# Fused cross-attention and layer norm: five tiles score q as projected, q's copies are issued early and then in one row, buffers of loads and stores are re-cut

## The reference

```
q = x @ wq;  k = ctx @ wk;  v = ctx @ wv            (split into 16 heads of 32)
scores = q . k / sqrt(32), masked with -inf where the mask is set
attn = softmax(scores) @ v
out = attn @ wo + x
result = (out - mean) / sqrt(var + 1e-5) * gamma + beta      (over the 512 columns)
```

## Time and profile before

| | |
|---|---|
| median of 3 runs | 668.11 us (665.15 to 670.7) |
| profiled execution, its own time | 671.11 us |
| its span in the trace | 668.9 us |
| PE busy | 619.7 us (93%) |
| DVE, ACT, POOL busy | 529.3, 507.7, 495.9 us |
| mean granted clock of TensorE | 0.977 |

### The profile page before, as it was taken

One profiled execution on the slowest core, in us unless ns is written; L12 is line 12 of the kernel. 1 busy time (PEld: TensorE's weight loads), 2 busy tenths in 40 slices (PEclk: granted clock), 3 DMA queues, 4 the chain that ended last, 5 costly groups with the idle time before them and its releaser, 6 DMA issues.

```text
span 668.9 us, 12812 instructions
## 1 busy us (share of the span) xinstructions
PE 619.7 (93%) x3836; PEld 481.1 (72%) x3836; DVE 529.3 (79%) x1007; ACT 507.7 (76%) x1558; POOL 495.9 (74%) x640
## 2 busy tenths in 40 slices
PE   7899499898998999999999999999999999999995
PEld 5667268586786868878786868777777868777663
DVE  5657359687787888888887889888888888888887
ACT  4757368687787878888887879888887879787761
POOL 6456336677696887979797887979797898867785
PEclk9799699999999999999999999999999999999999
DMA  8831725436264453717264453727273553727112
GB/s 293 229 97 20 190 58 138 130 102 185 78 174 153 111 157 95 221 57 220 87 182 145 122 147 113 203 65 219 80 195 121 140 147 96 210 88 188 34 48 111
DMA packets 56531, 91.14 MB, mean 136 GB/s; under 512 B 10896, under 2 KB 13968, under 8 KB 56464
## 3 DMA queue, kind: packets, MB, share of 16 engines
q1 hardware_dynamic: 56464, 90.32, 46.7%
HBM read 39.53 MB, written 16.78 MB: 84 GB/s over the span
## 4 chain that ended last, share of the span: by engine, by line
PE 44%; SPq 14%; DVE 14%; POOL 12%; DMA 7%; issue 5%; ACT 3%; POOLq 0%; DVEq 0%; ACTq 0%
PE bank L374 14%; PE bank L469 12%; SPq L280 10%; DMA qd<-qn 5%; PE bank L441 4%; PE bank L410 3%; PE bank L420 3%; POOL pn L888 3%; POOL y L912 3%; POOL y L914 3%; PE bank L396 2%; PE bank L446 2%; DVE pr L721 2%; DVE sm L734 2%; SPq L258 2%
## 5 line engine op out<-in xcount | busy, mean ns | idle before, releaser
L582 ACT ACTIVATE pr<-pr,nm 128x77 f32<-128x77 f32 x1024 | 269.9, 348 | 71.4 <-DVE nm L727 68.6
L888 POOL TENSOR_TENSOR pn<-pr,rec 128x512 f32<-128x512 f32 x128 | 134.9, 1054 | 117.4 <-DVE rec L736 110.5
L721 DVE SCALAR_TENSOR_TENSOR pr<-msk,bank 128x308 f32<-128x308 uint8 x256 | 111.0, 469 | 64.4 <-PE bank L410 49.9
L410 PE MATMUL bank<-kd,qd 128*128 128x154 f32 x480 | 85.9, 261 | 25.3 <-DMA qd<-qn 25.3
L469 PE MATMUL bank<-woh,ah 128*128 128x512 f32 x256 | 104.2, 407 | 3.7 <-DVE ql L709 2.3
L374 PE MATMUL bank<-xh,wqh 128*128 128x512 f32 x256 | 107.3, 419 | 0.0
L734 DVE TENSOR_REDUCE sm<-pr 128x8 f32<-128x616 f32 x128 | 99.7, 779 | 7.6 <-ACT pr L582 6.5
L727 DVE TENSOR_REDUCE nm<-pr 128x8 f32<-128x616 f32 x128 | 101.8, 795 | 4.4
L549 ACT ACTIVATE ptr<-bank 128x512 f32<-128x512 f32 (+1 forms) x256 | 95.7, 427 | 10.1 <-PE bank L420 9.9
L374 PE MATMUL bank<-xh,wql 128*128 128x512 f32 x256 | 102.3, 400 | 0.0
L374 PE MATMUL bank<-xl,wqh 128*128 128x512 f32 x256 | 102.3, 399 | 0.0
(11 more groups left out here) (75 smaller groups left out, 991.6 us busy)
## 6 DMA issues: line engine op xcount, KB each, us to landing
qd<-qn SPq DMA_DIRECT2D x240, 128.0 KB, 2.4
xraw<-xT SPq DMA_DIRECT2D x59, 256.0 KB, 3.0
xres<-x SPq DMA_DIRECT2D x58, 256.0 KB, 2.8
out<-y SPq DMA_DIRECT2D x56, 256.0 KB, 2.0
zt<-x SPq DMA_DIRECT2D x6, 256.0 KB, 3.9
out<-zt SPq DMA_DIRECT2D x6, 256.0 KB, 2.0
ptr<-xT SPq DMA_DIRECT2D x5, 256.0 KB, 9.0
kd<-kh SPq DMA_DIRECT2D x8, 154.0 KB, 3.6
```

What stands on the lines that cost most here:

```text
L410: last = nc.tensor.matmul(o[:, u * PW:(u + 1) * PW], qd[:, g, u, r * P:(r + 1) * P], kd[:, g, u, t // TB, :], start=False, stop=(u == 1))
L582: last = nc.scalar.activation(s, s, ACT.Exp, bias=nm[:, t % 2, h:h + 1], scale=1.0)
L721: nc.vector.scalar_tensor_tensor(out=pr[:, 4 * g:4 * g + 4, :], in0=msk[:, b % 2, t % TB, :].unsqueeze(1).broadcast_to([P, 4, LK]), scalar ...
L888: nc.gpsimd.tensor_tensor(pn[:, half, 0:4, :].rearrange("p s (e k) -> p (s e) k", e=2), pr[:, hs, 0:KM], rec[:, t % 2, hs].unsqueeze(2).br ...
```

## The change

- `kt` gets its own tile (`kt_sb`), placed so that it shares memory with the fourth group of `qd` and with `qn`. Its batch-0 part alone is cleared, by VectorE and not by GpSimd, and `pair_k` copies just the two blocks of 32 rows that hold data, with two transfers in place of one.
- Tiles 0 to 4 (PLAIN = 4) score q as projected. The four groups of block 1 are doubled one by one in SP's iterations 1 to 4 (DOUBLES), the fourth after tile 4's scores; for block 2 `keep_q` waits for tile 4's scores.
- From block 2 on all sixteen transfers of a block are issued in one row, after the load of a slice and before the store.
- NX goes from 3 to 2 and YS from 2 to 3. Slice t + 9 is loaded in iteration t. Slices 2 and 3 at the start go to other places.
- `place_v` is spread over iterations 0, 2, 4 and 5, one batch each. gamma and beta are loaded in iteration 5. The loads for the residual go ahead of `place_v` in iteration 5 and wait for the projection of v (`p_v`).
- The wait for the last of `place_v` moves from `project_o(0)` on TensorE to `standardise(0)` on ScalarE. `keep_q(3)` goes ahead of a slice and the first exponentials. `mask_all` runs in tiles with t % 16 = 1, before 2.

```diff
-NX = 3
-YS = 2
+NX = 2
+YS = 3
+
+PLAIN = 4
...
+DOUBLES = {1: 4, 2: 5, 3: 6, 4: 7}
+
-PLACE = {0: 0, 2: 1, 5: 2}
+PLACE = {0: (0, 0), 2: (1, 1), 4: (2, 1), 5: (3, 2)}
...
+            early("place_xres", [P, 4 * D - KT * NB * LK])
             vs = early("vs", [P, 3, 4, 2, 2, HD])
+        with ExitStack() as second:
+            second.enter_context(nc.sbuf_tensor("below_kt", [P, 6 * D], f32))
+            kt_sb = second.enter_context(nc.sbuf_tensor("kt_sb", [P, NB, NG, PW], f32r))
...
+        xres = sb("xres", [P, XR, D])
         y = sb("y", [P, YS, D])
-        xres = sb("xres", [P, XR, D])
...
                 sp.wait_ge(v_k, 4 * g + 4)
-                sp.dma_start(kd[64:128, g, 0].bitcast(f32), kt[0:64, g].bitcast(f32)).then_inc(d_kd[g], 16)
+                for j in range(2):
+                    sp.dma_start(kd[64 + 32 * j:96 + 32 * j, g, 0, :, j * LK:(j + 1) * LK].bitcast(f32),
+                                 kt[32 * j:32 * j + 32, g, :, j * LK:(j + 1) * LK].bitcast(f32)).then_inc(d_kd[g], 16)
...
-                sp.wait_ge(p_s, NG * (4 * blk - 1) + m + 1)
-                if i == 4:
-                    for g in range(NG):
-                        sp.wait_ge(d_kd[g], 48)
+                if blk > 1:
+                    sp.wait_ge(p_s, NG * (4 * blk - 1) + m + 1)
+                elif m == NG - 1:
+                    sp.wait_ge(p_s, NG * (PLAIN + 1))
                 sp.wait_ge(a_qh, i + 1)
...
-            for n in range(8, 11):
+            for n in range(8, 10):
                 load_slice(n)
...
             for t in range(T + LAG):
-                if t % 4 == 3 and t < T - 4:
-                    double_q(t + 1)
-                    double_q(t + 2)
-                if t >= 1 and t + 10 < 4 * NBLK:
-                    load_slice(t + 10)
+                if t >= 1 and t + 9 < 4 * NBLK:
+                    load_slice(t + 9)
+                if t in DOUBLES:
+                    double_q(DOUBLES[t])
+                if t % 4 == 3 and 3 < t < T - 4:
+                    for i in range(t + 1, t + 5):
+                        double_q(i)
+                if t == 5:
+                    sp.wait_ge(p_v, 3)
+                    for o in range(XR):
+                        load_res(o)
...
-                if t % 4 == 3 and t < T - 4:
-                    double_q(t + 3)
-                    double_q(t + 4)
...
-                if t == 7:
+                if t == 5:
                     sp.wait_ge(g_wo, 2 * KT)
                     sp.dma_start(gam[:], gamma.partition_broadcast(P)).then_inc(d_gb, 16)
...
-                if t == 5:
-                    sp.wait_ge(d_vm[1], 32 * 16)
-                    for o in range(XR):
-                        load_res(o)
...
-                    if blk == 0:
+                    if t <= PLAIN:
...
-                    if r == 0:
+                    if r == 0 or t == PLAIN + 1:
                         pe.wait_ge(d_qd[g], 64 * blk)
                         if blk == 1:
-                            pe.wait_ge(d_kd[g], 48)
+                            pe.wait_ge(d_kd[g], 64)
...
                 if t == 0:
                     pe.wait_ge(g_wo, 2 * KT)
-                    pe.wait_ge(d_vm[1], 32 * 16)
...
+                if i == 4:
+                    for g in range(NG):
+                        act.wait_ge(d_kd[g], 64)
+                if blk == 2:
+                    act.wait_ge(p_s, NG * PLAIN + m + 1)
                 if blk >= 2:
                     act.wait_ge(d_qd[m], 64 * (blk - 1))
...
+                if o == 0:
+                    act.wait_ge(d_vm[1], 32 * 16)
...
+            keep_q(3)
             keep_x(6)
             exps(0, 0)
-            keep_q(3)
...
-            dve.wait_ge(g_z, 2)
+            dve.wait_ge(g_z, 1)
+            dve.wait_ge(v_w, KT)
+            dve.wait_ge(p_k, NG)
+            nc.vector.memset(kt[:, :, 0, :].bitcast(f32), 0.0).then_inc(v_z, 1)
+            dve.wait_ge(v_z, 2)
...
-                if t % TB == 2:
+                if t % TB == 1:
                     mask_all(t // TB)
...
-            pool.wait_ge(v_w, KT)
-            pool.wait_ge(p_k, NG)
-            nc.gpsimd.memset(kt.bitcast(f32), 0.0).then_inc(g_z, 1)
```

More of the change, by code:

```diff
@@ L124, in cross_attention_layernorm @@
         z = sb("z", [P, 2, D])
+        xres = sb("xres", [P, XR, D])
         y = sb("y", [P, YS, D])
-        xres = sb("xres", [P, XR, D])
         ql = (ql0, ql1)
         qk = [ah] + [qn] * (NBLK - 1)
-        kt = qd[:].rearrange("p m u q -> p (m u q)")[:, 2 * NG * D - NG * NB * PW:].rearrange("p (g b k) -> p g b k", g=NG, b=NB)
+        kt = kt_sb[:].rearrange("p b g k -> p g b k")
         def x_of(n):
-            return (xraw[:, n] if n < NX else ptr[:, 0, 4, :] if n < KT else ptr[:, 1, n - KT, :] if n < 2 * KT
+            return (xraw[:, n] if n < NX else ptr[:, n - NX, 4, :] if n < KT else ptr[:, 1, n - KT, :] if n < 2 * KT
                     else xraw[:, (n - 2 * KT) % NX])
@@ L307, in _ @@
                 if t in PLACE:
-                    sp.wait_ge(a_v, PLACE[t] + 1)
-                    for b in ((0,), (1, 2), (3,))[PLACE[t]]:
-                        place_v(b)
+                    b, piece = PLACE[t]
+                    sp.wait_ge(a_v, piece + 1)
+                    place_v(b)
                 if t in (TB + 1, 2 * TB + 1):
@@ L397, in scores @@
                                      start=True, stop=False)
-                    if blk == 0:
-                        nc.tensor.matmul(o[:, 0:PW], qk[0][:, g, r * P:(r + 1) * P], kt[:, g, t // TB, :],
+                    if t <= PLAIN:
+                        nc.tensor.matmul(o[:, 0:PW], qk[blk][:, g, r * P:(r + 1) * P], kt[:, g, t // TB, :],
                                          start=False, stop=False)
-                        nc.tensor.matmul(o[:, 0:GW], qk[0][:, g, r * P:(r + 1) * P], kh[:, g, t // TB, :], start=False, stop=False)
-                        nc.tensor.matmul(o[:, PW:GW], qk[0][64:128, g, r * P:(r + 1) * P], kd[64:128, g, 1, t // TB, :],
+                        nc.tensor.matmul(o[:, 0:GW], qk[blk][:, g, r * P:(r + 1) * P], kh[:, g, t // TB, :], start=False, stop=False)
+                        nc.tensor.matmul(o[:, PW:GW], qk[blk][64:128, g, r * P:(r + 1) * P], kd[64:128, g, 1, t // TB, :],
                                          start=False, stop=True).then_inc(p_s, 1)
                         continue
-                    if r == 0:
+                    if r == 0 or t == PLAIN + 1:
                         pe.wait_ge(d_qd[g], 64 * blk)
                         if blk == 1:
-                            pe.wait_ge(d_kd[g], 48)
+                            pe.wait_ge(d_kd[g], 64)
                     for u in range(2):
```

## The result

The changed kernel took 644.13 us (median of 4 runs, 643.78 to 645.2), the kernel before 667.0 (4 runs, 665.15 to 670.7). The ratio is 0.9653, with a 95% interval of 0.9607 to 0.9699. The prediction had 639, 630 to 650, and 93% for faster. Between the two profiled executions the time went from 671.11 to 644.06 us and the span from 668.9 to 642.3.

The account below looks back on a forecast made before the run. TensorE, busy 93%, was the bound through idle time and low clock. Gains 4.6 + 11.7 + 3.0 + 11, less 1 and 0.5, made 28.8 us: 671.11 became 642.3, less 3.0 above the median: 639, range 630 to 650.

Parts of the forecast that it names:

- The start: TensorE's hole near 22.4 us and the low clock after it go: gain 4.6 us, bounds 2.4 and 4.9.
- Tile 4: Scoring q as projected needs no doubling, so tile 4 costs what tile 3 does plus 0.9 us: gain 11.7 us.
- gamma and beta: Issued in iteration 5, they arrive before tile 8, ending TensorE's al wait in tile 9: gain 3.0 of 3.3 us.
- The later blocks: Sixteen transfers in one row shrink TensorE's qd waits in 14 blocks: gain 11 us, bounds 4 and 15.9.
- under 5: Sign of being right: TensorE's waits for qd fall from 25.3 us to under 5.
- the row's length: In later blocks, sixteen issues on SP take 10.0 us, leaving a wait of about 0.2 to 0.25 us.
- Slice 15: SP is nearly full in the first tiles and two slice buffers leave nothing ready ahead: loss 0.5 us.
- The masks: VectorE's mask pass moves into a tile with weigh_v; three waits of 0.75 us may grow by 0.3: loss 1 us.
- 28.8: Sum of all gains and losses in us, taken from the profiled execution's 671.11 us.
- the 3.0 that I took off: The profiled execution stood 3.0 us above the median of 668.11, so 642.3 became 639 us.
- The rule of the Trainium skill: Rival: SP's issues in a row are cheap, so no qd wait is left in later blocks: 635.5 us, 5%.
- SP in the first tiles: Rival: SP becomes the bound in tiles 2 to 7, slices 12 to 15 come 2 to 3 us late: 646, 8%.

Follow-up runs that it names:

- e5: Changed kernel with the clearing of all of kt put back on GpSimd instead of VectorE: 647.11 us, ratio 0.9662.
- e4: Changed kernel with PLAIN = 3, so tile 4 scores from the doubled q again while the early doubling stays: 643.34 us, ratio 0.9601.
- e2: Changed kernel with gamma and beta issued in iteration 7 again, behind the doublings of block 2: 644.29 us, ratio 0.9634.
- e7: Changed kernel with the slice ahead of the doublings issued before the residual rows, in SP's iterations t % 4 = 2 from 6 on: 640.59 us, ratio 0.9582.
- e9: Changed kernel with every slice issued just ahead of a row of sixteen doublings loading 64 of its 512 columns: 640.69 us, ratio 0.9545.
- e1: Changed kernel with slice 15 issued ahead of place_v of batch 3 in SP's iteration 5: 641.98 us, ratio 0.9603.
- e11: Changed kernel run again with nothing altered, as the measure for the variants: 644.86 us (6 runs), ratio 0.9617 to the kernel before.
- e3: Changed kernel with the row of sixteen doublings split again around slice and store, from block 2 on: 652.32 us, ratio 0.972.

## Why the prediction was right, and where the 5 us went

*The start*: 4.6 forecast, 4.95 measured. The reason was the right one, and e5 shows both halves of it, the hole and the clock behind it, though only 3.0 us of it, as its hole was 1.25 us. In e0, the kernel before once more, the hole was 1.38 us, so the size of this term differs from execution to execution.

*Tile 4*: 11.7 forecast, 11.94 measured, with 0.49 us of wait for GpSimd where 0.9 had been put. e4 splits the reason, which the prediction gave as q as projected alone: 4.9 us are due to it, and 7.1 to the early doubling.

*gamma and beta*: 3.0 forecast, 3.35 of waiting measured, shown again by e2, and 1.2 us of low clock behind it that the sum had at nothing.

*The later blocks*: 11 forecast, 9.0 measured in waits (15.9 less 6.9, and not under 5 as the prediction had it for a sign), and 1.4 of low clock behind the wait of 2.83 us, again not in the sum. The step that was off is the row's length. I took it as twice the eight of the earlier trace rows, 10.0 us, and those eights have no slice directly ahead of them; the row has one, and took 10.1 to 11.7. e7 and e9 show that it can take 10.1 in nearly the same place.

*Slice 15*: 0.5 forecast, 2.8 measured (1.48 of wait, and an output projection of 4.3 us in place of 3.0); the 0.54 us for `qd` between them are in the 6.9 above. e1 gives 2.3 of it back. This is the term that was mis-sized most. The due times in the sum, 88 for the issue and 91 for the need, were right to 0.5 and 0.1 us, and with the median landing of 3.0 us of the kernel before they leave next to nothing to wait for; behind gamma and beta, two loads of 256 KB, the slice took 5.8, and in e2, without them, at most 3.4. And what stood behind ScalarE's wait, a clock that falls, was not in the sum at all.

*The masks*: 1 us more forecast, no change measured.

*Luck in the sum.* The end cost 1.6 us more, by a clock that fell in this execution. With it the parts add up to 27.4 us (4.95 + 11.94 + 4.55 + 10.4 - 2.8 - 1.6), of 26.6 in the span; 0.8 are not accounted for. That 28.8 comes so near is in part luck: 2.6 us of gain by the clock were left out, and so were 2.3 of the loss for slice 15 and the 1.6 at the end.

*From the execution to the number*: the gain between the two profiled executions was 27.05 us, where 28.8 was forecast. The rest of the 5 us is the 3.0 that I took off since the profiled execution of before stood above its median. The changed kernel's own did not stand above its median (644.06 and 644.13), so the difference was not a constant that both kernels share.

The rule of the Trainium skill ("DMA: Bandwidth & Descriptors", section "Issuing engines are not separate DMA queues"), that the time to start a DMA is "usually small relative to the DMA itself", was given 5% and would have led to 635.5. The rows of this case went the other way: 16 issues take 10.1 us at the least, and the landing 2.4. Of the rivals, SP in the first tiles is the one that was in part true: its load went out on time, but landed late, in one tile.

Not tested alone are two slice buffers in place of three, `place_v` spread over four iterations, and `keep_q(3)` moved ahead.

## What to carry to other kernels

When transfers feed an engine through one issuing queue, cost each by its place in that queue: the issue time of all ahead of it, whether a wait on another engine stands between, and how much is in flight when it starts. When a store moves behind a row of issues, ask whether its buffer has a spare: here, with the row in place, one more store buffer was worth 15 to 18 us, and with the buffer in place the row 5 to 8. A load that is moved up in the queue delays the ones behind it: gamma and beta, moved up, made the slice behind them land 2.4 us or more later. And read what a gain in one tile does to the next waits: in tile 4 a form of scores won 4.9 us and lost 3.3 of them in tiles 7 and 8, through one wait on SP.

## What the runs showed of the hardware

- Two executions of the changed kernel had the same wait of 1.39 us before the last two output projections. In the first the clock was low for the nine matmuls behind it (seven of them of 0.63 us) and the end took 13.3 us from there; in the second, e11, it took 11.8 (629.43 to 641.2). The kernel before had a wait of 1.42 and the full clock. In e3 a wait of 1.88 us for `qd` was followed by seven matmuls of 0.63 us, and the next block's, of 1.86, by none. So whether a hole of this length brings the lower level is not settled by its length.
- A 64-partition transfer of 128 KB takes 0.5 to 0.6 us to issue in a row. Rows of sixteen take 10.1 us at the least and up to 11.68 in the changed kernel, and the excess is in single issues of 0.7 to 1.9 us among others of 0.5 to 0.6. What makes them long is open.
